# Dividing the attention's results in four instructions of 256 columns instead of one of 1024, in a fused adaLN, attention and expert kernel

## The reference

```python
h = _layernorm(x, axis=-1) * (1 + ca) + sa
x = x + ga * _L0_attn_ref(h, L0_attn_W_qkv, L0_attn_b_qkv, L0_attn_W_o, L0_attn_b_o)
h = _layernorm(x, axis=-1) * (1 + cb) + sb
x = x + gb * _L0_ffn_ref(h, L0_ffn_gate_w, L0_ffn_w1, L0_ffn_w2)
```

```python
attn = jax.nn.softmax(scores + causal, axis=-1)
O = jnp.einsum('bhqk,bhkd->bhqd', attn, V)
O = O.transpose(0, 2, 1, 3).reshape(b, t, d)
return O @ W_o.T + b_o
```

## Time and profile before

| | |
|---|---|
| median of three runs | 998.71 us (998.51 to 1002.21) |
| span of the profiled execution, first to last instruction | 997.7 us; no device time of its own is listed, and the median stands 1.0 us above this span |
| PE busy | 902.3 us, 90% of the span |
| DVE busy | 718.0 us, 72% |
| ACT busy | 580.5 us, 58% |
| POOL busy | 357.4 us, 36% |
| line 883, the division on POOL | 7 instructions, 16.5 us |

### The profile page before, as it was taken

One profiled execution on the slowest core, in us unless ns is written; L12 is line 12 of the kernel. 1 busy time (PEld: TensorE's weight loads), 2 busy tenths in 40 slices (PEclk: granted clock), 3 DMA queues, 4 the chain that ended last, 5 costly groups with the idle time before them and its releaser, 6 DMA issues.

```text
span 997.7 us, 19445 instructions
## 1 busy us (share of the span) xinstructions
PE 902.3 (90%) x6174; PEld 531.5 (53%) x6174; DVE 718.0 (72%) x2323; ACT 580.5 (58%) x1271; POOL 357.4 (36%) x311
## 2 busy tenths in 40 slices
PE   5899899999899998999999897878899999999990
PEld 3543335433444443543443452423699899999980
DVE  8688766879656789757689669699638584444587
ACT  3335485776585777577666757567535433334562
POOL 1332020431321314333033454015386466565630
PEclk7899899999999999999999999999999999999995
DMA  8446436336326167251662745215313323222699
GB/s 282 127 65 129 61 81 144 59 44 146 63 35 133 42 112 142 69 76 59 106 115 85 152 64 189 73 27 174 96 53 123 95 70 106 78 75 71 198 309 306
DMA packets 83235, 110.61 MB, mean 111 GB/s; under 512 B 15930, under 2 KB 56434, under 8 KB 83138
## 3 DMA queue, kind: packets, MB, share of 16 engines
q1 hardware_dynamic: 75506, 89.45, 38.8%
q0 software_dynamic: 6816, 18.62, 6.1%
q10 hardware_dynamic: 816, 1.32, 0.4%
HBM read 69.42 MB, written 35.41 MB: 105 GB/s over the span
## 4 chain that ended last, share of the span: by engine, by line
PE 62%; DVE 16%; ACT 9%; issue 5%; DMA 4%; POOL 3%; SPq 1%; ACTq 0%; POOLq 0%; DVEq 0%
PE PO L1643 10%; PE PH L1520 9%; PE PY L1520 9%; PE PS L1623 8%; PE PM L1600 8%; ACT PR L1009 4%; DVE MXF L1322 3%; PE PHT L1728 3%; PE PX L1655 2%; PE PX L1569 2%; DVE JK L1319 2%; PE PS L1627 2%; PE PX L1578 2%; PE PX L1579 1%; ACT SF L992 1%
## 5 line engine op out<-in xcount | busy, mean ns | idle before, releaser
L1009 ACT ACTIVATE PR<-PS 128x512 f32<-128x512 f32 (+3 forms) x768 | 334.3, 497 | 142.4 <-PE PS L1627 108.1
L1319 DVE CUSTOM_DVE_ANT_0 JK<-PM,MK 128x128 bf16<-128x128 f32 (+3 forms) x512 | 239.1, 484 | 54.0 <-PE PM L1600 52.8
L1600 PE MATMUL PM<-QK 128*128 128x512 bf16 (+3 forms) x768 | 249.1, 333 | 23.4 <-DVE MXF L1322 15.0
L1623 PE MATMUL PS<-QK 128*128 128x512 bf16 (+3 forms) x768 | 247.5, 333 | 10.4 <-ACT PR L1009 7.4
L1322 DVE TENSOR_REDUCE MXF<-PM 128x1 f32<-128x512 f32 x256 | 175.1, 684 | 83.2 <-PE PM L1600 81.6
L1623 PEld LDWEIGHTS PS<-QK 128*128 128x128 bf16 x768 | 75.0, 98 | 170.4 <-ACT PR L1009 107.8
L1643 PE MATMUL PO<-PR,V 128*17 128x512 f32 (+3 forms) x1536 | 162.8, 496 | 0.0
L1600 PEld LDWEIGHTS PM<-QK 128*128 128x128 bf16 x768 | 75.5, 99 | 98.0 <-DVE MXF L1322 36.8
L1520 PE MATMUL PY<-W2S,HT 128*128 x852 | 118.9, 289 | 2.8 <-issue 1.9
L1520 PE MATMUL PH<-W1S,XT 128*128 x426 | 113.3, 402 | 0.9 <-DVE W2S L1474 0.9
L1627 PE MATMUL PS<-MT,identb 128*128 128x128 bf16 x512 | 111.9, 221 | 0.0
(11 more groups left out here) (269 smaller groups left out, 1194.9 us busy)
## 6 DMA issues: line engine op xcount, KB each, us to landing
QK<-SD SPq DMA_DIRECT2D x180, 128.0 KB
SD<-SP SPq DMA_DIRECT2D x42, 256.0 KB, 2.8
OP<-OS SPq DMA_DIRECT2D x64, 64.0 KB
LP<-LR SPq DMA_DIRECT2D x64, 64.0 KB
W1S<-in_w SPq DMA_DIRECT2D x8, 512.0 KB, 5.7
X<-XA SPq DMA_DIRECT2D x3, 1024.0 KB, 8.8
H2D<-XA SPq DMA_DIRECT2D x3, 1024.0 KB, 4.9
YG<-YT SPq DMA_DIRECT2D x12, 256.0 KB, 4.4
```

Source lines behind the costliest of these rows:

```text
L1009: eng.activation(PR[:, slot, i, c0:512], PS[m % 3][:, c0:512], ACT.Exp, scale=0.25).then_inc(S["exp"].sem, 1)
L1319: eng.tensor_tensor_reduce(JK[:, jk % 2, 0:w], PM[m % 3][:, 0:w], MK[:, 512 - w:512], 1.0, -3.0e38, ALU.add, ALU.max, MXA[:, mb, h, qt:qt ...
L1600: eng.matmul(PM[m % 3][:, 0:128 * (k1 - k0)], QK[:, r, h, 0, qt * 128:(qt + 1) * 128], QK[:, r, h, 1, k0 * 128:k1 * 128], start=True, stop ...
L1623: last = eng.matmul(PS[m % 3][:, c0:512], QK[:, r, h, 1, j * 128:(j + 1) * 128], QK[:, r, h, 0, 512 * f + c0:512 * f + 512], start=True, s ...
```

## The change

The division is cut in four steps (n = 0 to 3) of 256 columns. Step n covers the columns that step `out` with tp = n reads. They stand one and a half places apart in the list; those of unit 7 stand together. `out` waits for its own quarter, and the next unit's `lsum` waits for the last quarter.

```diff
-            place(*((2 * u + 2, 17) if u < 6 else (NG - 1, 6.5)), one("div", u))
+            place(*((2 * u + 2, 17) if u < 6 else (NG - 1, 6.5)), [(n and 1.5, ("div", u, n)) for n in range(4)])
...
-    place(4, one("div", 2 * B - 1))
+    place(4, [(0, ("div", 2 * B - 1, n)) for n in range(4)])
...
-                        sp.wait_ge(*after("div_d" if u - 1 == 6 else "div_p", "div", u - 1))
+                        sp.wait_ge(*after("div_d" if u - 1 == 6 else "div_p", "div", u - 1, 3))
...
-                    u = a[0]
+                    u, n = a
+                    part = slice(256 * n, 256 * n + 256)
                     po.wait_ge(*after("lrep", "lrep", u))
...
                     turn("div_p")
-                    eng.tensor_tensor(OP[:, u % 2, :], OP[:, u % 2, :], LP[:, :], ALU.mult).then_inc(S["div_p"].sem, 1)
+                    eng.tensor_tensor(OP[:, u % 2, part], OP[:, u % 2, part], LP[:, part], ALU.mult).then_inc(S["div_p"].sem, 1)
...
-                    eng.tensor_tensor(OP[:, u % 2, :], OP[:, u % 2, :], LP[:, :], ALU.mult).then_inc(S["div_d"].sem, 1)
+                    eng.tensor_tensor(OP[:, u % 2, part], OP[:, u % 2, part], LP[:, part], ALU.mult).then_inc(S["div_d"].sem, 1)
...
-                        pe.wait_ge(*after("div_d" if u == 6 else "div_p", "div", u))
+                        pe.wait_ge(*after("div_d" if u == 6 else "div_p", "div", u, tp))
```

More of the change, by code:

```diff
@@ L353 @@
     "lrep": {"lrep": 128},
-    "div": {"div_d": lambda u: int(u == 6), "div_p": lambda u: int(u != 6)},
+    "div": {"div_d": lambda u, n: int(u == 6), "div_p": lambda u, n: int(u != 6)},
     "bvb": {"bvb": 2},
```

## The result

The changed kernel takes 998.34 us (median of 20 runs, 994.87 to 1002.74) where the kernel before takes 1001.15 us (20 runs beside them, 995.97 to 1005.03). The ratio on record is 0.9969, with a 95% interval of 0.9957 to 0.9981 (the two medians alone give 0.9972): 0.31% less, within the 0.5% called no change. Two runs, both of the kernel before (1463 and 1751 us, beside the first four experiments), were slow ones and stand outside all ratios. The profiled execution has a span of 996.5 us; that of before had 997.7.

A forecast was written before the change was run, and what follows sets the result against it. PE, busy 90% of the span, was taken as the bound, idling behind DVE instructions held by POOL's division. Gains of 1.6 and 1.3 less 0.3 gave 2.6 us: 998.7 - 2.6 = 996.1 us, range 994.6 to 999.5.

The forecast's parts named there:

- Price of a quarter: A 256-column division on POOL takes 0.73 us (low end 0.59); four with gaps take 3.16 us against 2.36.
- The instruction gets into the gap: At units 1 and 3, DVE's held small instruction runs in the 0.08 us gap between two quarters on POOL.
- Rival A: DVE's instruction misses the gap and stays held until the third quarter ends, 2.35 us after the start: 999.0 us, chance 0.12.
- Unit 1: DVE's hold behind POOL's division ends 1.61 us sooner, and PE, idle 1.88 us there, gains 1.6 us.
- Unit 3: DVE's hold behind POOL's division ends 1.63 us sooner; PE gains 0.9 to 1.6 us, counted as 1.3.
- under 0.5 was to show it: Sign: PE's idle time ahead of the first output falls from 1.88 and 1.74 us to under 0.5 us.
- Unit 6: The division on DVE, which is the chain there, takes 1.42 us in quarters against 1.13: 0.3 us later.
- Unit 5: DVE has only work out of PSUM during POOL's division, so nothing is held and nothing gained.
- Units 0, 2, 4 and 7, and the fourth quarter: Cost nothing: POOL's pauses cover the quarters, the fourth fits into 1.47 us idle; unit 7 costs 0.5 us without cover.
- rival C: POOL's queue becomes the bound at the outputs, each fourth quarter adding 0.81 us in three batches: 1001.4 us, chance 0.07.
- so the finer wait of `out` frees nothing by itself: PE starts the first output behind a division without having waited for it, so waiting for one quarter gains nothing by itself.
- rival B: Holds shorten, but what follows waits for something no sooner (a DRAM transfer, ACT); all taken back: 999.0 us, chance 0.13.

The follow-up runs named there:

- the first four experiments: Four of the follow-up runs, measured side by side with the kernel before, which had 999.67 us there (35 runs of it).
- together_last: Changed kernel, but all four quarters stand at the whole division's place and every `out` waits for the last quarter: 999.24 us, ratio 0.9971 to the kernel before.
- together: Changed kernel, but all four quarters stand at the whole division's place, `out` still waiting for its own quarter: 995.53 us, ratio 0.9976 to the kernel before.
- stats_early: Kernel before, division whole, with the batches' statistics (DVE's small instructions) four places earlier: 1003.03 us, ratio 1.0042 to the kernel before.
- others_only: Changed kernel with quarters for units 0, 2, 4, 6 and 7 only, division whole at units 1, 3 and 5: 1003.72 us, ratio 1.0035 to the kernel before.

## Why the prediction was right, and where it was not

- **Total.** Forecast 2.6 us less, 0.26%; measured 0.31% [0.19, 0.43] and 0.33% [0.11, 0.54]. It counts as no change, as was said. The time itself, 998.34 us, lies inside the range of 994.6 to 999.5 but 2.2 us above the forecast of 996.1, because the three runs that the forecast started from lay low.
- **Price of a quarter.** 0.73 us taken, 0.729 measured; the gap is 0.07 to 0.08. The product `TM<-G,BO` of the same shape was the right row, and a plain quarter of 2.36 us (0.59) too low.
- **The instruction gets into the gap.** It did at units 1 and 3, each time within 0.03 us behind the quarter's end. Rival A is out: the held instructions last 0.24 to 0.56 us. The figure that the prediction weighed for A (115 ns, in the Trainium skill, SBUF — State Buffer, section on SBUF's two separate sides) is for a GpSimd transfer that waits for DVE; here DVE waits for GpSimd, and it is done 0.02 to 0.03 us behind the end of a quarter.
- **Unit 1.** 1.6 us counted, 1.8 measured in its stretch (11.1 to 9.3). The second small instruction was held too, as was said, and lasts 0.41 us, but it comes ahead of the reduction that PE needs and not behind it (256.50 and 256.96). It costs nothing all the same, because PE is busy until then: its matmul has no idle time ahead of it.
- **Unit 3.** 1.3 us counted within 0.9 to 1.6; 1.5 measured, with 0.52 us of idle time left, where under 0.5 was to show it.
- **Unit 6.** 0.3 us counted, 0.1 measured in the stretch and 1.32 - 1.13 = 0.19 on the chain: a piece has 0.33 us there, not 0.355. The rule of the Trainium skill (VectorE: DVE Perf Modes, the TRN2 errata) gave an estimated 0.47; the trace disagrees with it, with 0.19.
- **Unit 5.** Nothing is held there, as was said, but the reading behind it is wrong. DVE does not have "only work out of PSUM" while the division runs from 576.92 to 579.28. In DVE's timeline of before it also has instructions of 8 columns from SBUF to SBUF, and they run in their usual time:

```profile
577.12 0.16 DVE L1372 FIND_INDEX8 I<-V,LG 128x8 uint32<-128x8 f32 x1
```

  So "a small DVE instruction on SBUF data that cannot run while POOL's runs" is too wide: it depends on the instruction.
- **Units 0, 2, 4 and 7, and the fourth quarter.** Cost nothing, says the prediction. For the fourth quarter that is shown (0.71 to 0.73 us of idle time left, ended by ACT), so rival C is out. For units 0 and 2 the stretches show it, within 0.1 us. For units 4 and 7 it is not shown.
- **The steps that failed.** First, "so the finer wait of `out` frees nothing by itself". It stands as far as it goes, but the prediction stopped there: once PE is early, the division becomes what it waits for (1.40 us in together_last). It is the finer wait that keeps unit 1's gain whole, as together shows, where all four quarters stand ahead of the output. Second, the sum had no term for DVE's `recip`. It gave back 0.9 to 1.1 us at unit 1 in these profiles, and why the transfer came late is open. So rival B, "what follows waits for something that does not come sooner (a transfer on its way through DRAM)", was right in kind for about a third of the gain, though the transfer stands ahead of the held instruction, not behind it.
- **Right by compensation, in part.** The two holds gave 3.3 us where 2.9 were counted, and `recip` took about 1.0 that was not counted. Another 0.5 to 0.8 us came between 170 and 182 (31.47 and 31.80 us in the profiles of before, 30.98 and 30.97 in those of the changed kernel). There PE waits 0.56 and 0.90 us for a transfer (`QK<-CD`) in before and not at all in the changed kernel; kernels with the cut have from nothing to 0.85 us of this wait and up to 31.75 us, so the cut alone does not explain it. In all 60 to 182 gives 2.7 to 2.9 us, and unit 6 takes 0.1 of it. That this sum meets the forecast of 2.6 is luck in part. Beyond 182 the profiles scatter more than these terms.

## What to carry to other kernels

A long POOL instruction on SBUF data can cost more than its own time: in these runs it held DVE's small products and scalings (TENSOR_TENSOR and TENSOR_SCALAR, 8 columns, 0.16 us by themselves) until it ended. Look in the timeline for DVE instructions of a few columns that last over 0.5 us, and read what ended at their end. Then see whether PE waits behind them; only such holds are worth anything. Cutting the long instruction bounds the hold by one piece and keeps the order of all other steps nearly as it is, at 0.26 us a piece on POOL (0.18 fixed and a gap of 0.08). Moving the small ones can bring them under another POOL instruction, and the version that did so took 0.4% more here. Where one engine's wait is shortened, look which wait ends next (POOL's division at together_last, `recip` in DVE's order), and give the readers the finer wait with the cut.

## What the runs showed of the hardware that was not expected

- A gap of 0.07 us between two POOL instructions is enough for a held DVE instruction. At units 1 and 3 in the changed kernel and in window 8 of stats_early nine were held; each ended 0.02 to 0.03 us behind the end of a POOL instruction, and behind seven of them the next POOL instruction started within 0.07 to 0.15 us of the last one's end. All 104 instructions of 8 columns that lasted over 0.2 us beside a product or sum on POOL, in the 14 profiles, ended 0.02 to 0.03 us behind the end of one, and none was held over two.
- Not only products of two inputs are held: single-source instructions of 8 columns, float32 and int32, were (lines 1262, 1266, 1269 and 1280 above), while reductions and copies out of PSUM ran beside POOL in their usual times. But not every instruction from SBUF to SBUF is held either: FIND_INDEX8 (43 times), MAX8 (50 times) and BATCH_NORM_STATS2 (95 times) ran wholly within such a POOL instruction in 0.17, 0.16 and 0.43 us at most.
- Behind idle time of PE that a hold had caused, the granted clock was found at 0.50 for about 3 us (others_only) and about 10 us (stats_early), with matmuls at 3.39 us instead of 1.95; behind as much idle time in three other profiles it stayed at 1.00. Such stretches are not tied to the division: the kernel before has them in other places, as here behind a wait of PE for DVE (PE's timeline and the windows' table of before):

```profile
624.39 0.75 PE L1664 MATMUL PX<-ident,XA 128*128 128x128 f32 x4 [1.44 <-DVE CT L1350]
...
624.00:626.00 2.00, 1.60 (x12) 0.57 (x12) 0.25 (x2) 0.60 (x1) 0.00 (x0) 0.69 1.03 347
626.00:628.00 2.00, 2.00 (x12) 0.54 (x5) 0.02 (x1) 0.44 (x1) 0.00 (x0) 0.50 0.23 55
```

  A profile that shows a hold without this shows its lower price.
- Four instructions of 256 columns cost DVE 1.32 us on the chain where one of 1024 costs 1.13.
